# Pacing the gathers of tile 0 by their landings in place of memsets

## The reference

```python
e = jnp.stack([tbl_0[ids[:, 0]], ..., tbl_38[ids[:, 38]]], axis=1)      # (2048, 39, 32)
p = e[:, ROW, :]                      # ROW, COL: the 741 pairs i < j
q = e[:, COL, :]
z = jnp.einsum('bpc,apc,bpa->bp', p, w, q)
h = jnp.concatenate([z, dense_ctx], axis=1)
h = jnp.maximum(h @ W_top1 + b_top1, 0.0)
h = jnp.maximum(h @ W_top2 + b_top2, 0.0)
y = h @ W_top3
```

## Time and profile before

| | us |
|---|---|
| median of 3 runs | 795.97 |
| lowest, highest run | 794.8, 798.86 |
| the profiled execution's own time | 796.05 |
| its span, first to last instruction | 794.2 |
| PE busy | 732.0 (92%) |
| DVE busy | 637.3 (80%) |
| POOL busy | 422.5 (53%) |
| ACT busy | 104.3 (13%) |
| POOL's gathers, 384 | 379.3, mean 988 ns |
| POOL's memsets, 75 | 43.3, mean 577 ns |
| mean granted TensorE clock | 0.974 of full |

### The profile page before, as it was taken

The page is one execution under the profiler, slowest core; times in us unless marked ns, Lnnn a source line. Parts: engine busy times, 40 slices in busy tenths (PEclk is TensorE's granted clock), DMA queues, the critical chain, the costliest instruction groups (busy, mean ns, idle before and its releaser), DMA issues.

```text
span 794.2 us, 11392 instructions
## 1 busy us (share of the span) xinstructions
PE 732.0 (92%) x4418; PEld 291.8 (37%) x4418; DVE 637.3 (80%) x797; ACT 104.3 (13%) x186; POOL 422.5 (53%) x463
## 2 busy tenths in 40 slices
PE   1688686999979999999999999999999999999998
PEld 0232222333333344444333444444333443443343
DVE  4658698999978999878978898879969887778650
ACT  3232111011100010101111010110111010011002
POOL 6899999943556555545556555455656455100000
PEclk9879798999999999999999999999999999999999
DMA  7544429587888636356765555347765455443300
GB/s 213 167 149 157 125 88 299 207 293 260 282 293 289 224 99 232 97 187 191 251 214 163 193 166 190 117 154 234 232 219 168 144 158 181 163 144 92 116 1 0
DMA packets 71553, 142.02 MB, mean 179 GB/s; under 512 B 13301, under 2 KB 22600, under 8 KB 71372
## 3 DMA queue, kind: packets, MB, share of 16 engines
q1 hardware_dynamic: 49228, 118.04, 43.4%
q10 hardware_dynamic: 9984, 16.94, 6.0%
q0 software_dynamic: 12288, 6.32, 5.3%
HBM read 110.25 MB, written 31.00 MB: 178 GB/s over the span
## 4 chain that ended last, share of the span: by engine, by line
PE 74%; DVE 11%; issue 6%; DMA 4%; POOL 3%; ACT 2%; SPq 1%; ACTq 0%; DVEq 0%
PE z_ps L610 24%; PE u_ps L586 23%; PE t_ps L549 10%; PE m_ps L623 8%; DVE prod L910 6%; DVE one_hot L898 4%; POOL e_rows L409 3%; PE m_ps L625 3%; PE t_ps L530 2%; DMA scratch<-parts 1%; DMA e<-scratch 1%; PE u_ps L645 1%; PE u_ps L654 1%; PE m_ps L627 1%; PE m_ps L637 1%
## 5 line engine op out<-in xcount | busy, mean ns | idle before, releaser
L910 DVE TENSOR_TENSOR prod<-u_ps,eT 128x1024 f32<-128x1024 f32 x400 | 469.9, 1216 | 96.0 <-PE u_ps L586 95.4
L409 POOL DMA_INDIRECT e_rows<-in_tbl_dram,idx x384 | 379.3, 988 | 257.5 <-DVE prod L910 184.9
L586 PE MATMUL u_ps<-e,w 128*128 128x512 f32 x800 | 256.5, 434 | 21.9 <-DVE prod L910 11.6
L610 PE MATMUL z_ps<-prod,sel 128*32 128x512 f32 x1600 | 262.8, 612 | 0.0
L586 PEld LDWEIGHTS u_ps<-e,w 128*128 128x128 f32 x800 | 133.2, 190 | 160.8 <-DVE prod L910 76.7
L549 PE MATMUL t_ps<-one_hot,tb 125*32 125x512 bf16 x1560 | 155.0, 398 | 14.4 <-DVE one_hot L898 14.2
L898 DVE TENSOR_SCALAR one_hot<-hot_idx,row 125x512 bf16<-125x512 f16 (+2 forms) x320 | 137.1, 482 | 11.4 <-PE t_ps L549 9.5
L549 PEld LDWEIGHTS t_ps<-one_hot,tb 125*32 125x32 bf16 x1560 | 55.9, 99 | 112.1 <-issue 68.0
L610 PEld LDWEIGHTS z_ps<-prod,sel 128*32 128x32 f32 x1600 | 43.8, 109 | 139.7 <-issue 108.8
L623 PE MATMUL m_ps<-zT,w1s 128*128 128x512 f32 x144 | 73.5, 592 | 0.0
L714 ACT CAST parts<-t_ps 128x512 fp32r<-128x512 f32 (+1 forms) x40 | 23.4, 586 | 238.1 <-PE t_ps L549 144.1
(11 more groups left out here) (53 smaller groups left out, 133.1 us busy)
## 6 DMA issues: line engine op xcount, KB each, us to landing
w<-w_rows SPq DMA_DIRECT2D x100, 512.0 KB, 5.9
e<-scratch SPq DMA_DIRECT2D x62, 512.0 KB, 4.8
scratch<-parts SPq DMA_DIRECT2D x62, 256.0 KB
w_rows<-h ACTq DMA_DIRECT2D x48, 256.0 KB
e_rows<-in_tbl_dram,idx POOLq DMA_INDIRECT x384
hot_idx<-hot SPq DMA_DIRECT2D x12, 512.0 KB
h<-in_w_dram ACTq DMA_DIRECT2D x12, 256.0 KB, 3.7
e<-scratch SPq DMA_DIRECT2D x8, 384.0 KB, 4.2
```

Of the source, the lines that this page charges most:

```text
L409: pool.indirect_dma_start(e_rows[:, r, n, D * q:D * q + D], None, tables[f], bass.IndirectOffsetOnAxis(ap=idx[:, t, f * TPG + n:f * TPG + ...
L586: last = nc.tensor.matmul(u_ps[:, s % 2, place, :], w4[:, p % WR, (u % PW) * P:(u % PW + 1) * P], e4[:, E4_SLOT[g], j - C * g, :], start=T ...
L610: last = nc.tensor.matmul(z_ps[D * quad:D * quad + D, z % 2, :], sel[:, D - 1 - row:2 * D - 1 - row], prod[:, (NS * t + n) % PR, place, :] ...
L910: nc.vector.tensor_tensor(prod[:, s % PR, :, :], u_ps[:, s % 2, :, :], e, ALU.mult).then_inc(s_mul, 1)
```

## The change

Gathers 20 to 95 no longer have a memset behind them. Instead each waits, before it is issued, until the gather two ahead of it in line has landed (`WINDOW = 2`). So that a count can tell of one gather's landing, each buffer's semaphore is split in two, for gathers of even and of odd number: of gathers 20 to 95, at most one that adds to a given semaphore is in flight. `turn` on PE then waits for both counts. SP's wait for the memsets is dropped. The paced part, from gather 96 on, keeps its rule. Line numbers of the new kernel are two or three lower or higher from here on (the gather is at 412, the transpose at 528).

```diff
--- before.py
+++ after.py
@@ -167,13 +167,18 @@
 
 
 
-PAUSES = PACED_FROM - 1 - sum(TPG * len(gathered(c)) for c in GATHERED[:2])
-
-
-def rows_count(c):
-
-    n = GPOS[c]
-    return sum(16 * TPG * len(gathered(GATHERED[x])) for x in range(n % ER, n + 1, ER))
+WINDOW = 2
+GATHERS = [c for c in GATHERED for k in range(TPG * len(gathered(c)))]
+
+
+def landed(n):
+
+    return 16 * len([m for m in range(n % WINDOW, n + 1, WINDOW) if (GPOS[GATHERS[m]] - GPOS[GATHERS[n]]) % ER == 0])
+
+
+def last_gathers(c):
+
+    return [max(n for n in range(w, len(GATHERS), WINDOW) if GATHERS[n] == c) for w in range(WINDOW)]
 
 
 def stores_to(n):
@@ -308,9 +313,6 @@
         y_sb = h1[0:1, 0, :]
 
 
-        pause = w1s[:, 0, :]
-
-
         zroom = zT[:, 1, :, :].rearrange("p k n -> p (k n)")
         hroom = h1[:, :, :].rearrange("p m n -> p (m n)")
         w_in_room = [hroom[:, k * NB:(k + 1) * NB] for k in range(2)]
@@ -360,7 +362,7 @@
         s_wlo = sem("s_wlo")
         s_wout = [sem(f"s_wout{r}") for r in range(2)]
         s_w4 = [sem(f"s_w4{r}") for r in range(WR)]
-        s_rows = [sem(f"s_rows{r}") for r in range(ER)]
+        s_rows = [[sem(f"s_rows{r}_{w}") for w in range(WINDOW)] for r in range(ER)]
         s_tp = sem("s_tp")
         s_eh = sem("s_eh")
         s_et = sem("s_et")
@@ -380,7 +382,6 @@
         s_m = sem("s_m")
         s_mc = sem("s_mc")
         s_y = sem("s_y")
-        s_pause = sem("s_pause")
 
         def e_slot(t, g):
             return NG + TWO_PLACES.index(g) if t % 2 and g in TWO_PLACES else g
@@ -394,7 +395,6 @@
         @block.gpsimd
         def _(pool):
             pool.wait_ge(s_idx, 16)
-            paused = 0
             issued = 0
             for c in GATHERED:
                 t, g = c
@@ -404,18 +404,16 @@
                 for q in gathered(c):
                     f = C * g + q
                     for n in range(TPG):
+                        if GPOS[c] > 1 and issued < PACED_FROM:
+                            before = issued - WINDOW
+                            pool.wait_ge(s_rows[GPOS[GATHERS[before]] % ER][before % WINDOW], landed(before))
                         if issued >= PACED_FROM:
                             pool.wait_ge(s_mul, issued - PACE_LEAD + 1)
                         pool.indirect_dma_start(
                             e_rows[:, r, n, D * q:D * q + D], None, tables[f],
                             bass.IndirectOffsetOnAxis(ap=idx[:, t, f * TPG + n:f * TPG + n + 1], axis=0),
-                        ).then_inc(s_rows[r], 16)
+                        ).then_inc(s_rows[r][issued % WINDOW], 16)
                         issued += 1
-                        if GPOS[c] > 1 and issued < PACED_FROM:
-                            if paused:
-                                pool.wait_ge(s_pause, paused)
-                            nc.gpsimd.memset(pause[:, :], 0.0).then_inc(s_pause, 1)
-                            paused += 1
 
         @block.sync
         def _(sp):
@@ -495,7 +493,6 @@
             for t in range(NT):
                 for b in range(NBAT):
                     if t == 0 and b == MLP_WEIGHTS_BATCH:
-                        sp.wait_ge(s_pause, PAUSES)
                         for dst, src in ((w1s[:, :, :], w1), (w2s[:, :, :], w2), (w3s[:, :], w3), (b1s[:, :], b1), (b2s[:, :], b2)):
                             sp.dma_start(dst, src).then_inc(s_mlpw, 16)
                     for c in COMPLETE.get(NBAT * t + b - 1, ()):
@@ -520,7 +517,8 @@
                 last.then_inc(s_idt, 1)
 
             def turn(c):
-                pe.wait_ge(s_rows[GPOS[c] % ER], rows_count(c))
+                for n in last_gathers(c):
+                    pe.wait_ge(s_rows[GPOS[c] % ER][n % WINDOW], landed(n))
                 if POS[c] > 0:
                     pe.wait_ge(s_et, POS[c])
                 lo, hi = D * gathered(c)[0], D * (gathered(c)[-1] + 1)
```

## The result

The changed kernel takes **788.53 us** (median of 4 runs, 787.02 to 790.31), the kernel before beside it on the same chip 797.08 (4 runs, 794.8 to 798.86). The ratio is **0.9895**, with an interval of 0.9869 to 0.9922: 1.05% faster. The forecast was 788.0. The profiled execution took 790.31 us with a span of 788.4 and a granted clock of 0.976; before it was 796.05, 794.2 and 0.974.

What follows compares the result with a forecast made beforehand. Between 35 and 168 us it took DVE as the bound in C, DVE and PE side by side in E, and the load of e in D. 2.3 + 3.8 + 1.9 = 8.0 off 796.05 gave 788.0 us, range 780.5 to 796.5.

Steps and rivals of the forecast that it cites:

- The memsets' price on DVE: Between 35 and 168.5 us, memsets lengthen DVE's one_hot comparisons by 14.5 us in all, 32% of their time there.
- A: Stretch from 35 to 63.2 us: two comparison blocks on the chain of waits, 7.04 us, save 32%, 2.3 us.
- C: Stretch from 96 to 120.7 us, bound by DVE: all of its comparisons' saving counts, 3.8 us.
- B: Stretch from 63.2 to 96 us: worth nothing, since DVE is idle 9.5 us and waits for PE and ACT.
- E: Stretch from 132 to 168.5 us: 3.8 us possible, but PE's idle 1.9 us limits the saving to 1.9.
- D: Stretch from 120.7 to 132 us: worth nothing; PE's 6.0 us wait for the load of e only moves forward.
- swallowed in D: Weight traffic sets when the load of e lands, its wait grows by 6.1 us: 794.1 us. Chance 0.15.
- The wait on the gather two ahead: POOL's gathers 20 to 95: costs nothing, starts 1.65 us apart, last near 157 us, slack 38 us at chunk 6's turn.
- All of it counts: Rival: B, D and E give their share too, all 14.5 us saved: 781.6 us. Chance 0.12.
- Too late: Rival: gathers start 2.46 us apart, PE waits 16.1 us at chunk 6's turn in tile 0: 812.2 us. Chance 0.04.
- A gather holds DVE as a memset does: Rival: each of 81 comparisons meets a gather and loses 0.94 us, 34 us on the path: 830 us. Chance 0.02.
- The change doesn't bind: Rival: the landing wait may never hold, leaving only the memsets' removal; same time as the forecast, no separate chance.

Runs made afterwards that it cites:

- Both: The changed kernel with the 75 memsets put back behind gathers 20 to 94, the landing wait kept: 798.12 us, ratio 0.9995.
- before, SP's order: The kernel before, memsets kept, with w and the hot indices of batch 10 issued behind the load of e in batch 11: 797.22 us, ratio 0.9995.
- one in flight: The changed kernel with one gather in flight in place of two (WINDOW = 1): 878.55 us in a single execution.
- the change again: The changed kernel run once more with nothing altered, beside the kernel before: 790.11 us (6 runs), ratio 0.9907.

## Why the prediction was right, and where its terms were off

**The memsets' price on DVE: right.** 14.5 us were worked out of the earlier trace rows. By the means of the three shapes the comparisons lost 46 x 173 + 18 x 213 + 17 x 147 ns = 14.3 us between the same places of the program. "Both" brings the price and the time of before back, so that the memsets are the cause is shown. The price isn't all held by the memsets themselves: 6.3 us of it stand at gathers, and vanish with the memsets all but 0.8.

**A, 2.3 us: near.** The window shows 1.6. From that first block of comparisons (33.28, now 32.86) to the multiplications of the second batch (63.13, now 60.54) it went from 29.85 to 27.68 us, 2.2 less. **C, 3.8 us: right in this pair**, 3.6; in the table the column 12-22 shrinks by 2.0 to 2.4 in all eight profiles without memsets. The other 1.5 of C lie in the column 2-12, which scatters: 34.58 in this profile of the change, 36.66 in the next, against 36.32 before. So it was in part this execution's luck. **B, nothing: right**, 0.2.

**E, 1.9 us: too large**, 1.3. The cover was rightly named, since PE has 0.8 us idle there, but not all of its idle time could be had. In the table the column 28-44, which lies mostly in E, gives 1.5 to 1.8 against the kernel before (and 0.8 to 1.0 against "before, SP's order").

**D, nothing: the step that failed.** I wrote that the wait "is only moved forward". It grew by 1.8 us in the profiled execution, the load of e from 6.72 to 8.29. That is the second rival (swallowed in D), true for a part: of the 5.8 us that A and C gave it took 1.8, not all. How much of it belongs to the change is open. The five profiles without memsets and with SP's order unchanged have waits of 5.07, 6.10, 6.87, 7.78 and 7.83 us in D, 6.7 on average; the five with memsets of any size (one of them with SP's order altered) have 5.41 to 5.97, 5.7 on average. So D takes back about 1 us, with a scatter larger than that.

**The median came out at the forecast partly by offsets.** In the two profiled executions the sum of the terms is -1.0 (before A) -1.6 -0.2 -3.6 +1.8 -1.3 = -5.9, against a forecast of -8.0. The medians differ by 8.55. The profiled execution of the change is the slowest of its four (790.31), and the change again has a median of 790.11; its ten executions lie between 787.02 and 792.23, with a median of 789.8. The forecast of 788.0 lies at the good end of what the change does. Some 0.6 us of the -1.0 ahead of A is also the memsets': the first one (34.71) lengthened a comparison that began at 34.34, just ahead of my cut at 35.

**The wait on the gather two ahead: cost right, size wrong.** I took a mean distance of 1.65 us and the last start at 157; they are 1.93 and 177.90. The step that failed is "in quiet time the wait costs nothing". It set 2.44 us, the time in which the rows land, against two starts of 1.25. But with one in flight two starts are 2.80 us apart, since the 2.44 runs to the landing and not to POOL's next start: half of 2.80, 1.40, was the figure for quiet time, and not 1.25. The slack on chunk 6 was not 38 us: gather 87 starts at 156.22, gather 89, which waits for it, at 163.10, and the turn is at 181.10, 18 us later. The cost stays nothing, since 18 is enough, but half of the cover that I named wasn't there. At 2.22 us the cover would have been gone, and "one in flight" shows how steep it is behind that: 81 us.

**The rivals.** "All of it counts" (781.6) fell: over the whole stretch DVE now waits 11.1 us for PE's u_ps (6.3 before), B gave only 0.2, and E is at PE. "Too late" didn't come at two in flight and did at one. "A gather holds DVE as a memset does" (830) fell by its price, but not in kind: a gather does hold a comparison, for 90 to 250 ns and five times in the changed kernel, and not for 0.94 us each time. "The change doesn't bind" fell too, since 51 of 76 starts waited, although its time would have been the same.

**The rule on the lock.** The row: a comparison that begins just behind a memset takes 821 ns in place of 468, and a comparison at a memset is lengthened by 345 ns on average, most of a memset's 577. The Trainium skill ("SBUF — State Buffer", section "Who interferes with whom") says that who "issues first gets the shared pair for the whole instruction". For memsets the trace agrees, down to the pair above, where DVE's end comes 0.28 us behind the memset's. The section says it of DVE's 2-port modes. No row prints a comparison's mode; its cost, (611 - 354) / 1024 = 0.25 ns a column against prod's 1217 / 1024 = 1.19, fits a faster one. The prediction also had the trace agree on operations with two inputs. That is no test of it: the section's sentence is about two inputs in SBUF, and prod reads one of its two, u_ps, from PSUM. What the rows show is that the memsets leave prod alone (1210 ns beside them, 1214 without).

By the letter a gather would hold the pair for its whole instruction too, and there the measurement decides: it does so for a part. In the changed kernel the five lengthened comparisons were, 0.2 us after their start, in the last 0.11 to 0.28 us of a gather, and stayed until it had ended. Of 36 comparisons that were further from a gather's end none was lengthened by more than 20 ns. That is why the mean is 349 ns with 76 gathers beside it. The hold goes both ways: a gather that met no comparison took POOL 0.94 us and the longest 1.77, a memset 0.54 and 0.85.

**Left open:** how much of D's growth is the change's; whether waiting for landings is worth anything over no pacing at all (0.9895 and 0.9907 against 0.9921 and 0.9918); whether SP's order is worth 1 us; the one execution of 2406.61 us; and why gathers hold comparisons for longer and more often when full memsets stand between them than with memsets on one partition, or with none. A pacing by something that POOL does outside SBUF wasn't tried.

## What to carry to other kernels

A filler instruction that paces one engine isn't free because nobody waits for that engine: compare the mean durations of the other engines' instructions, by shape, in stretches with and without it, look at single pairs before you say who holds whom (the means of the changed kernel hid five comparisons held by gathers), and count only what lies in stretches where that engine or its consumer is the bound. When transfers are limited by a number in flight, take the distance between two starts with one in flight from start to start, semaphore included, and not from the landing alone. And repeat an execution before reading a few us of one transfer as a cause: one wait of 3.8 us looked like a fix, and was 5.5 the next time.

## What was not expected of the hardware

- A memset on one partition takes POOL 552 ns, on 128 partitions 577. The columns decide (256 columns: 362 ns). These means hold the memsets that DVE held up; the medians are 516, 543 and 331 ns.
- A gather holds a DVE comparison near its end: with memsets between the gathers, 20 comparisons ended 0.12, 0.25 or 0.38 us (by their shape) behind the end of a gather.
- With one in flight, two gathers of 128 rows start 2.80 us apart in quiet time. In the quiet stretches two in flight still waited for up to 3.2 us (the gather of 51.45), and in D for 5.73.
- The load of e took between 4.79 and 8.29 us in kernels that differ in nothing ahead of it but the order of two transfers; the same kernel, run again, took 6.65 instead of 4.79.
